# Cross attention: every fourth low half of the probabilities on GpSimd instead of VectorE

## What is computed

```python
qh = (q @ wq.T).reshape(B, Sq, N_HEADS, HEAD_DIM).transpose(0, 2, 1, 3)
kh = (k @ wk.T).reshape(B, Sk, N_HEADS, HEAD_DIM).transpose(0, 2, 1, 3)
vh = (v @ wv.T).reshape(B, Sk, N_HEADS, HEAD_DIM).transpose(0, 2, 1, 3)
scores = jnp.einsum('bhqd,bhkd->bhqk', qh, kh) / jnp.sqrt(jnp.float32(HEAD_DIM))
attn = jax.nn.softmax(scores, axis=-1)
ctx = jnp.einsum('bhqk,bhkd->bhqd', attn, vh)
ctx = ctx.transpose(0, 2, 1, 3).reshape(B, Sq, N_HEADS * HEAD_DIM)
return ctx @ wo.T
...
x = x + _L1_xattn_ref(_layernorm(x, axis=-1), ctx_1024, ctx_1024, L1_xattn_wq, L1_xattn_wk, L1_xattn_wv, L1_xattn_wo)
```

## Time and profile before

| | |
|---|---|
| median of 3 runs | 4021.47 us |
| the profiled execution: its own time | 4028.95 us |
| its span | 4027.2 us |
| busy PE | 3254.7 us (81%) |
| busy DVE | 2787.4 us (69%) |
| busy ACT | 2233.2 us (55%) |
| busy POOL | 808.2 us (20%) |
| mean granted clock of TensorE | 0.91 |

### The profile page before, as it was taken

How to read it: one execution, slowest core, us unless ns; L and a number is a source line. 1 busy time by engine, 2 the same in 40 slices (tenths; PEclk the granted TensorE clock), 3 DMA queues, 4 the chain that set the end, 5 groups by cost and what they waited for, 6 DMA issues and landing times. The chain is left out here.

```text
span 4027.2 us, 80612 instructions
## 1 busy us (share of the span) xinstructions
PE 3254.7 (81%) x31163; PEld 1896.3 (47%) x31312; DVE 2787.4 (69%) x4071; ACT 2233.2 (55%) x4222; POOL 808.2 (20%) x1397
## 2 busy tenths in 40 slices
PE   6999999968999744799868888988798879988533
PEld 2636363645666433455434554555454544554211
DVE  4727272676877566444368997799778987899488
ACT  2717171665766421333247886688668876788111
POOL 1101010032321033122012232122312232222112
PEclk9999999979999867899979999999899989999855
DMA  2010101042131146122169999999999999999532
GB/s 105 2 64 2 64 10 34 23 179 95 40 122 43 69 167 213 70 71 73 39 166 199 188 193 185 214 191 195 193 214 186 195 189 191 194 194 191 131 125 83
DMA packets 1198255, 513.85 MB, mean 128 GB/s; under 512 B 1102380, under 2 KB 1103404, under 8 KB 1195832
## 3 DMA queue, kind: packets, MB, share of 16 engines
q1 hardware_dynamic: 1194664, 496.14, 56.2%
q0 software_dynamic: 3216, 12.58, 0.9%
HBM read 168.87 MB, written 65.01 MB: 58 GB/s over the span
## 5 line engine op out<-in xcount | busy, mean ns | idle before, releaser
L1874 DVE SCALAR_TENSOR_TENSOR ca_halves<-ca_probs,ca_inv,ca_halves 128x1024 f16<-128x1024 f32 x512 | 654.6, 1278 | 171.5 <-ACT ca_halves L1803 166.8
L1803 ACT ACTIVATE ca_halves<-ca_probs,ca_inv 128x1024 f16<-128x1024 f32 x512 | 585.8, 1144 | 164.3 <-DMA ca_pt<-ca_halves 159.3
L1868 DVE TENSOR_REDUCE ca_neg_max<-banks 128x1 f32<-128x1024 f32 x512 | 622.3, 1216 | 62.2 <-PE banks L1688 61.9
L1795 ACT ACTIVATE ca_probs<-banks,ca_neg_max 128x1024 f32<-128x1024 f32 x512 | 568.1, 1110 | 100.0 <-DVE ca_neg_max L1868 97.6
L1688 PE MATMUL banks<-ca_kt,ca_qt 64*128 64x512 f16 x3072 | 395.1, 392 | 137.4 <-ACT ca_probs L1795 127.3
L1708 PE MATMUL banks<-ca_pt,ca_v 128*64 128x256 f16 x6144 | 397.1, 281 | 10.4 <-DMA ca_pt<-ca_halves 8.6
L1708 PEld LDWEIGHTS banks<-ca_pt,ca_v 128*64 128x64 f16 x6144 | 325.1, 112 | 119.3 <-issue 99.4
L1649 POOL TENSOR_SCALAR ca_inv<-ca_total 128x1 f32<-128x1 f32 x512 | 100.0, 195 | 1166.8 <-ACT ca_probs L1795 1164.8
L1688 PEld LDWEIGHTS banks<-ca_kt,ca_qt 64*128 64x128 f16 x3072 | 135.4, 96 | 332.7 <-issue 128.2
L1652 POOL TENSOR_TENSOR ca_inv<-ca_inv,ca_minus_one 128x1 f32<-128x1 f32 x512 | 281.8, 550 | 42.6
L589 ACT ACTIVATE ba_probs<-banks,ba_neg_max 128x256 f32<-128x256 f32 (+1 forms) x512 | 194.5, 476 | 99.8 <-DVE ba_neg_max L611 98.9
(11 more groups left out here) (330 smaller groups left out, 5643.9 us busy)
## 6 DMA issues: line engine op xcount, KB each, us to landing
ca_w<-ca_w_parts SPq DMA_DIRECT2D x32, 768.0 KB, 5.3
wa_x<-in_x SPq DMA_DIRECT2D x32, 256.0 KB, 5.0
wa_ring<-in_x SPq DMA_DIRECT2D x32, 256.0 KB, 3.0
x_after_window_attention<-wa_ring SPq DMA_DIRECT2D x32, 256.0 KB, 2.0
ba_x<-x_after_window_attention SPq DMA_DIRECT2D x32, 256.0 KB, 5.3
ba_kt_stage<-in_ctx_t SPq DMA_DIRECT2D x4, 2048.0 KB, 8.4
ba_v_stage<-in_ctx SPq DMA_DIRECT2D x4, 2048.0 KB, 13.7
ba_ring<-x_after_window_attention SPq DMA_DIRECT2D x32, 256.0 KB, 3.0
```

Source lines behind the costliest of these rows:

```text
L1795: act.activation(probs[:, slot, :], scores(i), ACT.Exp, bias=neg_max[:, slot:slot + 1], accum_out=total[:, slot:slot + 1]).then_inc(exped, 1)
L1803: act.activation(halves[:, slot, 0, :], probs[:, slot, :], ACT.Copy, scale=inv[:, slot:slot + 1]).then_inc(split_hi, 1)
L1868: dve.tensor_reduce(out=neg_max[:, slot:slot + 1], in_=scores(i), axis=X_AXIS, op=ALU.max, negate=True).then_inc(maxed, 1)
L1874: dve.scalar_tensor_tensor(out=halves[:, slot, 1, :], in0=probs[:, slot, :], scalar=inv[:, slot:slot + 1], in1=halves[:, slot, 0, :], op0= ...
```

## The change

Items with i % 4 = 1 (one item in four, 128 of 512, always the second of an even step) have their low half made by POOL. POOL has no single operation for it in this kernel: `low_half` on POOL first scales the probabilities in place (probs = probs x inv), waits for its own semaphore `split_scaled`, and then subtracts the high half. It runs right behind POOL's reciprocal of item i + 1, and begins with a wait for the high half of item i. DVE leaves these items out. SP before its transpose, and ACT before it overwrites the probabilities, wait on the semaphore of the engine that made the low half (`wait_split`).

```diff
--- before.py
+++ after.py
@@ -1515,7 +1515,8 @@
         v_projected, v_hi, v_lo = sem("ca_v_projected"), sem("ca_v_hi"), sem("ca_v_lo")
         scored, maxed, exped = sem("ca_scored"), sem("ca_maxed"), sem("ca_exped")
         minus_filled, shrunk, inverted = sem("ca_minus_filled"), sem("ca_shrunk"), sem("ca_inverted")
-        split_hi, split_lo = sem("ca_split_hi"), sem("ca_split_lo")
+        split_hi, split_lo, split_pool = sem("ca_split_hi"), sem("ca_split_lo"), sem("ca_split_pool")
+        split_scaled = sem("ca_split_scaled")
         turned = [sem(f"ca_turned{i}") for i in range(SLOTS)]
         weighted, ot_hi, ot_lo = sem("ca_weighted"), sem("ca_ot_hi"), sem("ca_ot_lo")
         xh_hi, xh_lo = sem("ca_xh_hi"), sem("ca_xh_lo")
@@ -1550,6 +1551,17 @@
         tile_at = {tile_step(b, t): (b, t) for b in range(B) for t in range(NT)}
         store_at = {step + 2: tile for step, tile in tile_at.items()}
         reload_at = {step + 3: tile for step, tile in tile_at.items()}
+
+        def on_pool(i):
+
+            return i % 4 == 1
+
+        def wait_split(engine, i):
+
+            if on_pool(i):
+                engine.wait_ge(split_pool, i // 4 + 1)
+            else:
+                engine.wait_ge(split_lo, i + 1 - (i + 2) // 4)
 
         def turned_by(i):
 
@@ -1620,7 +1632,7 @@
                             sp.wait_ge(weighted, (step - 4) // 2 + 1)
                         for h in range(2):
                             i = 2 * step + h
-                            sp.wait_ge(split_lo, i + 1)
+                            wait_split(sp, i)
                             sp.dma_start_transpose(pt[:, step % 4, h, :, :],
                                                    halves[:, i % SLOTS, :, :].rearrange("p q s -> p (q s)")
                                                    ).then_inc(turned[i % SLOTS], 16)
@@ -1638,6 +1650,15 @@
 
             @block.gpsimd
             def _(pool):
+                def low_half(i):
+                    slot, mine = i % SLOTS, i // 4
+                    pool.wait_ge(split_hi, i + 1)
+                    pool.tensor_scalar(probs[:, slot, :], probs[:, slot, :], inv[:, slot:slot + 1], 1.0,
+                                       ALU.mult, ALU.mult).then_inc(split_scaled, 1)
+                    pool.wait_ge(split_scaled, mine + 1)
+                    pool.tensor_tensor(halves[:, slot, 1, :], probs[:, slot, :], halves[:, slot, 0, :],
+                                       ALU.subtract).then_inc(split_pool, 1)
+
                 pool.memset(minus_one[:, :], -1.0).then_inc(minus_filled, 1)
                 pool.wait_ge(minus_filled, 1)
                 for step in range(STEPS):
@@ -1650,6 +1671,8 @@
                                            ALU.mult, ALU.mult).then_inc(shrunk, 1)
                         pool.wait_ge(shrunk, i + 1)
                         pool.tensor_tensor(inv[:, at], inv[:, at], minus_one[:, :], ALU.pow).then_inc(inverted, 1)
+                        if i >= 1 and on_pool(i - 1):
+                            low_half(i - 1)
                     if s == STATS_AT + NT + 2 and b + 1 < B:
                         norm_gpsimd(pool, n, b + 1)
                     ready = norm_tile(step - 1)
@@ -1791,7 +1814,7 @@
                     slot = i % SLOTS
                     act.wait_ge(maxed, i + 1)
                     if i >= SLOTS:
-                        act.wait_ge(split_lo, i - SLOTS + 1)
+                        wait_split(act, i - SLOTS)
                     act.activation(probs[:, slot, :], scores(i), ACT.Exp, bias=neg_max[:, slot:slot + 1],
                                    accum_out=total[:, slot:slot + 1]).then_inc(exped, 1)
 
@@ -1906,7 +1929,7 @@
                         maximum(2 * step + 1)
                     if step % 2 == 1 and 5 <= step <= LAST - 1:
                         out_low((step - 5) // 2)
-                    if 1 <= step <= STEPS:
+                    if 1 <= step <= STEPS and not on_pool(2 * step - 1):
                         low_half(2 * step - 1)
                     if step >= 1:
                         low_item(step - 1)
```

## The result

The changed kernel took 4077.25 us (median of 4, 4074.73 to 4083.4) against 4022.92 for the kernel before (median of 4): a ratio of 1.0141, interval 1.0116 to 1.0166. The kernel is slower by 54 us; 4061 was forecast, with 4020 to 4130 as the range of its own case. The profiled execution took 4083.4 us (span 4081.7), 54.5 more than that of before. It lies in cross attention: its first high half starts 0.6 us earlier than before and its last at 3802.1 instead of 3745.1.

What follows compares the result with a forecast made beforehand. No single engine bound it; the three-slot loop's latency counted. Quiet pairs 25, crowded 30 and 9, less 25 of relief: net +39, say +40, on 4029 gives 4069, 4061 in the runs' terms; own range 4020 to 4130, 8-in-10 3975 to 4390.

Steps and rivals of the forecast that it cites:

- The loop of three slots: Cross attention: high half, low half, transpose (4.6 us to landing in the median), then high half of i+3.
- T: Time from the end of the high half to the low half done: about 3.3 us instead of 1.3.
- (a) and (b): POOL, 1024 columns: (a) subtraction, 2.13 us; (b) scaling by one pointer and one immediate, 1.06 us, at most 3.97.
- the second rival: The pointer makes POOL's scaling slow, 3.97 us, T = 7.4: +350, 4379 us profiled, 4371 in the runs' terms; chance 0.27.
- the third: Half-way rival, one pointer costing half of two: scaling 2.5 us, T = 4.7, 166 more, 4230 us; chance 0.08.
- The relief: 128 low halves, 164 us, leave DVE; less idle on PE and ACT gives back 25 us.
- The exponential of i+3: On ACT, it needs the slot of the probabilities: ready at 2761.5 against 2761.30, 0.2 us late.
- The reciprocal behind the queue: POOL's reciprocal of i+2 queues behind the two operations: costed at nothing, up to half a microsecond where ACT runs closer.
- The high half of i+3: On ACT, 1.2 us late behind the transpose; the output copy's 1.10 us wait for PE covers all but 0.1 to 0.3.
- quiet pairs: 83 pairs of steps, 25 us; 45 crowded ones, where context, normalised rows and output tiles also pass, cost 30 and 9.
- rival 1: DVE was the bound and its relief wins: 3984 us profiled, 3976 in the runs' terms; chance 0.25.
- The exclusion: POOL's subtraction and DVE's low half of i+1 shut each other out: 0.3 us of lateness, which relieved DVE can bear.

Runs made afterwards that it cites:

- the series of T: Changed kernel with POOL's low half as one memset (3998.97 us), the subtraction alone (4023.01 us), three memsets (4063.57 us), or as in the change (4077.25 us).
- The kernels at 2.2 and 3.4 us with the same reads: Changed kernel with POOL's scaling moved ahead of the high half, only the subtraction behind it: 4034.44 us; and the changed kernel itself: 4077.25 us.
- the single memset: Changed kernel with POOL's low half replaced by one memset writing zeros: 3998.97 us, ratio 0.9931 against the kernel before.
- The memset series: Changed kernel with POOL's low half replaced by one memset of zeros (3998.97 us) or three in a row (4063.57 us).
- the early scaling: Changed kernel with POOL's scaling right after the reciprocal, before the high half: 4034.44 us, ratio 1.0017 against the kernel before.
- both places that looked free by it: Changed kernel moving items with i % 4 = 0 (4096.82 us, ratio 1.0185) or i % 4 = 3 (4132.81 us, ratio 1.0277 against the kernel before).

## Why the prediction was right, point by point

- **The sign, and its reason.** Right. The loop of three slots decides, not DVE's load. Shown by the series of T, all with the full relief: 1.1 us -24, 2.2 us 0, 3.1 us +40, 3.4 us with reads +54. The kernels at 2.2 and 3.4 us with the same reads differ by some 40 (4034 and 4077; up to 12 of it can be ACT's shorter high half). In this series POOL's queue is taken for longer as T grows. With the reciprocal out of that queue the loss is still 52 us, so it does not need the queue.
- **(a) and (b), the operations.** Right: 2.129 and 1.121 us against 2.13 and 1.06. The scalings of 4 us, the second rival, did not come, nor the third (whose sum takes 1.4 us late and multiplies by 1.3; nothing hangs on it).
- **The relief, taken at 25.** 24 by the single memset. DVE's busy time fell by 100 us in the stage and not by 164, because 384 low halves were 128 ns longer, 49 us. The other 15 us I did not trace; part is that busy time counts an overlap of neighbours once, and a low half ends 0.08 us after the start of what follows it.
- **The exponential of i+3, "0.2 us late".** Mis-sized. It waits 73.8 us over the stage, 0.58 for each moved item and 0.91 in the pair shown. T was 3.4, not 3.3, and ACT came to the exponential 2.6 us behind the high half in that pair, not 3.1 as in the earlier trace rows, where 0.18 us of waiting for the maximum is included and another 0.18 for PE. I took the time of need from the trace of before with its waits in it; that the relief takes these away is argued from two pairs, not tested.
- **The reciprocal behind the queue, "I cost it at nothing here".** The step that failed: 66 waits, 37.9 us. I had counted 0.9 us of room for its two operations (0.19 and 0.55 us) and not that the first reads SBUF and would meet DVE's low half: 1.05 us. How much of the +54 it is stays open, since taking it away moved the wait to the transposes.
- **The high half of i+3, covered by PE in quiet pairs, dear in crowded ones.** Wrong in its second half. The crowded pairs were to give 39 of 64 us gross; there the wait for transposes grew by 3.4 us and the time by 6.7. The quiet pairs were to give 25 gross and gave 50.9 net of the relief, 0.6 us a pair. That PE's 1.10 us would cover is borne out in kind: the wait for the weighing fell by 43.7. But in the quiet pairs it did not hold the loss to 0.3.
- **The sign "if the wait for transposes does not grow, my case is wrong and rival 1 right".** It can't tell the two apart. That wait grew by 36 us in the change, short of the 50 named, and by 38 with the single memset, where rival 1's mechanism wins by 24 us.
- **The exclusion, 0.3 us of lateness for DVE.** Right in size and in kind: 49 us over 128 moved items are 0.38 us each. The Trainium skill has the condition (SBUF — State Buffer, "Who interferes with whom"): a DVE operation with two SBUF inputs contends with a POOL operation that reads SBUF, not with one that only writes. The traces agree on both sides, 1281 ns beside memsets and 1394 to 1406 beside scalings and subtractions.
- **The sum, +40.** +54 measured. That the total came so near is in part luck: the crowded pairs were priced too high, the quiet ones too low, the reciprocal at nothing and the exponential at a fraction, and these errors largely cancel. I take the 14 us to be the last two, less what their waits covered of others; that is argued and not shown. The memset series has the same 14 us between T = 3.1 without reads and the change.

## What to carry to other kernels

Work moved to an idle engine is priced by its latency in the loop that it stands in, not by its busy time: here each moved item freed 1.28 us of DVE and yet lost time, because the low half took 3.4 us in a ring of three slots. What can be done ahead of the critical hand-over should be (the early scaling gave back some 40 of 54 us, up to 12 of them perhaps by ACT's quicker copy), and small operations behind a long one on an in-order queue need their own line in the sum. Read the time of need in a trace as one that will move, and be wary of slack read off one pair of steps: both places that looked free by it cost more than the change's own.

## What the runs showed of the hardware that was not expected

- A POOL scaling with one pointer and one immediate runs at the quick rate, 1.121 us for 1024 columns; the slow neighbour of the earlier trace rows has a subtraction and two pointers.
- POOL's one-column operation took 1.05 us instead of 0.19 when DVE's low half was running, and behind memsets up to 1.25. When POOL and DVE both read, the turns passed from one to the other in the pair shown: 1.49 us for the low half, then 1.05 us for the POOL operation behind it. DVE's low half took up to 2351 ns.
- ACT's copy of 1024 columns to f16 takes 1.05 us with an immediate scale and 1.14 with a pointer, in the kernel that scales early.
